# A Mamba layer pair of two batches as one pipeline of eight half-sequence items, in a decoder layer kernel

## The chip, the cores and the metric

One core of one Trainium2 chip runs the whole decoder layer as one program. The metric is the time of one execution on the device in microseconds. The engines are named as the profile names them: PE (TensorE, matrix products and transposes), PEld (its weight loads), DVE (VectorE), ACT (ScalarE), POOL (GpSimd) and SP (SyncE, which only issues transfers here). SBUF is the on-chip memory, PSUM the accumulators of PE (eight banks of 512 float32 per partition).

## What is computed

Four batches of 1024 tokens by 256 features in float32. Each batch goes through two Mamba blocks, a memory attention, a normalisation, a cross-attention over 64 context tokens, another normalisation, and then all batches together through a top-2-of-8 mixture of experts with a last normalisation. What the change touches is the Mamba block and what surrounds it:

```python
def mamba_block(x, in_w, in_b, conv_w, conv_b, xp_w, dt_w, dt_b, A_log, D_ssm, out_w, out_b):
    xz = x @ in_w.T + in_b                      # 256 -> 2 x 512
    xm, res = jnp.split(xz, 2, axis=-1)
    xc = causal depthwise convolution of xm, 4 taps
    xm = silu(xc + conv_b)
    x_dbl = xm @ xp_w.T                         # 512 -> 64 + 16 + 16
    delta = softplus(x_dbl[..., :64] @ dt_w.T + dt_b)
    Bm, Cm = x_dbl[..., 64:80], x_dbl[..., 80:]
    # per token, for 512 channels x 16 states:
    #   h = h * exp(delta * A) + delta * xm * Bm ;  y = sum over states of h * Cm
    y = (y + xm * D_ssm) * silu(res)
    return y @ out_w.T + out_b
out1 = mb(rmsnorm(x, norm1_w));  x1 = x + out1
out2 = mb(rmsnorm(x1, norm2_w)); out2 = memory_attend(out2, ...)
return x1 + out2
```

## The kernel before

Every engine runs its own list of instructions in order, and semaphores tie the lists together; no scheduler reorders anything. The four batches run one after the other. For each, `mamba(b, m)` runs twice (m is the layer), then come the memory attention and the cross-attention, and after the last batch the experts.

A call of `mamba` has three parts. The **preparation** works on all 1024 tokens: the root mean square (L705, L694), scaling (L1308), transposes of the normalised input (L920, drained at L682), the input product (L926), the first convolution tap on ACT (L729) and three on DVE (L1316) out of an SBUF copy `pre`, Silu (L722), the product to rank and B, C (L973), the product to delta (L980), softplus as Abs, Exp, Ln (L745 to L764) with a series for small arguments shared by POOL (L569, L573) and DVE (L1332 to L1351), the product delta times xm (L1327) and its transposes (L998, drained at L799).

The **scan** has 128 chunks: 2 halves of 512 tokens, 16 states, 4 groups of 128 channels. For each state `spread_b` multiplies the transposed delta times xm by B (three of four token tiles on ACT, L779, one on POOL, L582). For each chunk, `fill` transposes 4 tiles into a bank of `psD` (PE, L1012), `decay` computes exp(delta A) into `da_ring` (ACT, L786), DVE scans (L1363) into `h_ring`, POOL multiplies by the broadcast row of C (`weigh_c`, L597), and `add_y` transposes and accumulates in `psA` (PE, L1032). `psD` and `psA` have four banks each, `da_ring` and `h_ring` eight places. `open_y` starts each half's accumulation with 16 products by the diagonal of D_ssm (L1022), after ACT has copied the previous half out (`keep_y`, L792). In the first half POOL also keeps the last state of each chunk (L593).

The **end** transposes y back (L1056), gates it (Silu at L828, product at L1373), and multiplies by out_w (L926, then L1382 or L1385 on DVE).

## Time and profile before

| | us |
|---|---|
| median of 3 runs | 3635.7 (3633.0 to 3639.06) |
| the profiled execution | 3660.78 |
| its span, first to last instruction | 3659.0 |
| busy: PE, DVE, ACT, POOL | 2742.5, 2217.9, 1904.8, 1665.2 |

The span is about 2 us shorter than the profiled execution, which itself is 25 us above the median. Busy time of PE is modelled with overlapping records, so what PE can really issue is read from the distance between starts, not from the mean of one matmul. A line's idle time names whom the engine waited for. The timeline merges equal neighbours; four merged instructions of 0.71 us that span 2.55 us start every 0.61 to 0.64 us.

### The profile page before, as it was taken

The page shows a single profiled execution, that of the slowest core. Times are in us where ns is not written, and L with a number is a line of the kernel's source. Part 1 is how long each engine was busy: PE and PEld are TensorE (multiplying, and loading weights), DVE is VectorE, ACT ScalarE, POOL GpSimd, SP SyncE. Part 2 cuts the span into 40 slices and gives each one's busy share as a digit, 9 for nine tenths or more (in the row PEclk, how much of TensorE's full clock was granted, in tenths as well). Part 3 has the DMA queues.
Part 4 walks back from the last instruction along what each step waited for, and adds up shares of the span by engine and source line. Part 5 has one row for each costly group of instructions (what it writes and reads, how often), then busy time and mean ns, then how long its engine had stood idle before and what let it go on. Part 6 is the DMA issues. An engine that isn't in the chain of part 4 may idle for free.

```text
span 3659.0 us, 44328 instructions
## 1 busy us (share of the span) xinstructions
PE 2742.5 (75%) x15274; PEld 2050.4 (56%) x15275; DVE 2217.9 (61%) x2787; ACT 1904.8 (52%) x3028; POOL 1665.2 (46%) x1723
## 2 busy tenths in 40 slices
PE   5787688877777896687688867777895299999910
PEld 2674576547647754674676547647754166666600
DVE  4894893468668645894893468678643033333347
ACT  5785781378678525785781378678531011111100
POOL 2792791039639602792791039639602501000060
PEclk9898899889989998898899889989996599999955
DMA  5110120001001100110110001001102212111031
GB/s 197 43 51 1 41 64 1 12 18 52 25 18 50 38 1 13 44 50 1 44 61 1 12 18 53 24 18 53 35 1 102 81 62 90 62 63 62 33 93 47
DMA packets 91235, 158.84 MB, mean 43 GB/s; under 512 B 14130, under 2 KB 39986, under 8 KB 91058
## 3 DMA queue, kind: packets, MB, share of 16 engines
q1 hardware_dynamic: 72338, 106.80, 9.4%
q0 software_dynamic: 15392, 47.99, 3.6%
q8 instruction: 104, 1.70, 0.2%
...
q14 instruction: 73, 0.60, 0.1%
...
## 4 chain that ended last, share of the span: by engine, by line
PE 41%; POOL 30%; DVE 11%; issue 8%; ACT 7%; DMA 2%; another core or an unknown queue 1%; DVEq 0%; POOLq 0%; SPq 0%; ACTq 0%
POOL arena L597 25%; PE psD L926 13%; PE psD L1237 7%; PE psA L926 6%; POOL arena L582 4%; PE psD L1114 2%; PE psA L1089 2%; PE psD L1135 2%; DVE arena L1351 2%; PE psA L973 2%; PE psA L1228 1%; DVE arena L1349 1%; PE psA L920 1%; ACT arena L779 1%; DVE arena L1338 1%
## 5 line engine op out<-in xcount | busy, mean ns | idle before, releaser
L597 POOL TENSOR_TENSOR arena<-arena 128x512 f32<-128x512 f32 x1024 | 1091.2, 1092 | 10.7 <-POOL carry L593 0.5
L1012 PE MATMUL psD<-ident,arena 128*128 128x128 f32 x4096 | 651.6, 286 | 274.6 <-ACT arena L779 209.9
L1012 PEld LDWEIGHTS psD<-ident,arena 128*128 128x128 f32 x4096 | 479.1, 146 | 374.0 <-ACT arena L779 273.5
L786 ACT ACTIVATE arena<-arena,negA 128x512 f32<-128x512 f32 x1024 | 662.1, 712 | 12.2 <-DVE arena L1363 11.4
L1363 DVE TENSOR_TENSOR_SCAN arena<-arena,psD 128x512 f32<-128x512 f32 x512 | 581.7, 1200 | 137.8 <-PE psA L1032 81.4
L1032 PE MATMUL psA<-ident,arena 128*128 128x128 f32 x4096 | 617.7, 274 | 19.0 <-POOL arena L597 18.7
L1363 DVE TENSOR_TENSOR_SCAN arena<-arena,carry,psD 128x512 f32<-128x512 f32 x512 | 602.4, 1255 | 37.0 <-PE psA L1032 37.0
L779 ACT ACTIVATE arena<-arena,bc 128x512 f32<-128x512 f32 x768 | 498.0, 712 | 87.4 <-PE psD L1012 86.3
L1032 PEld LDWEIGHTS psA<-ident,arena 128*128 128x128 f32 x4096 | 479.1, 142 | 32.3 <-POOL arena L597 32.3
L926 PE MATMUL psD<-arena 128*128 128x512 f32 (+4 forms) x776 | 336.9, 569 | 43.5 <-POOL strip L545 28.7
L883 ACT ACTIVATE in_w_sb<-in_w_sb 128x512 f32<-128x512 f32 x140 | 88.1, 630 | 457.6 <-DVE in_w_sb L1559 457.6
L926 PE MATMUL psA<-arena,in_w_sb 128*128 128x512 f32 x512 | 251.0, 650 | 84.1 <-ACT bc L769 84.1
L639 POOL DMA_DIRECT2D ys_dram<-arena x70 | 38.0, 543 | 532.8 <-DVE arena L1570 525.1
L682 ACT ACTIVATE arena<-psA 128x512 f32<-128x512 f32 x160 | 90.3, 597 | 319.9 <-PE psA L1089 117.2
L1237 PE MATMUL psD<-arena 128*128 128x256 f32 x1120 | 254.2, 380 | 2.9 <-DVE arena L1565 2.9
L573 POOL TENSOR_TENSOR arena<-arena 128x1024 f32<-128x1024 f32 x32 | 88.2, 2757 | 357.5 <-ACT arena L750 357.5
L1559 DVE TENSOR_TENSOR in_w_sb<-psD,arena 128x512 f32<-128x512 f32 x140 | 96.8, 692 | 244.6 <-PE psD L926 244.6
L582 POOL TENSOR_SCALAR arena<-arena,bc 128x512 f32<-128x512 f32 x256 | 177.0, 692 | 118.1 <-ACT arena L799 118.1
L926 PEld LDWEIGHTS psD<-arena 128*128 128x128 f32 (+1 forms) x776 | 143.1, 194 | 150.8 <-issue 140.7
L926 PEld LDWEIGHTS psA<-arena,in_w_sb 128*128 128x128 f32 x512 | 105.6, 211 | 217.5 <-issue 124.2
L1237 PEld LDWEIGHTS psD<-arena 128*128 128x128 f32 x1120 | 207.3, 190 | 30.1 <-DVE arena L1565 4.8
L555 POOL TENSOR_TENSOR arena<-arena,out_b_sb 128x2048 f32<-128x2048 f32 x4 | 18.0, 4496 | 373.4 <-DMA x_dram<-arena 373.4
...
## 6 DMA issues: line engine op xcount, KB each, us to landing
arena<-c_dram SPq DMA_DIRECT2D x256, 256.0 KB, 3.2
...
arena<-xs_dram SPq DMA_DIRECT2D x71, 128.0 KB
ys_dram<-arena POOLq DMA_DIRECT2D x70, 128.0 KB, 2.0
...
```

The source lines that it names most:

```text
L573: pool.tensor_tensor(series[:, f, :], series[:, f, :], soft_e[:, f, :], ALU.mult)\
L582: pool.tensor_scalar(g[:, v % 2, JS, :], uT[:, t, :], bc[:, t, n:n + 1], 1.0, ALU.mult, ALU.mult).then_inc(b_by_pool, 1)
L597: pool.tensor_tensor(h_ring[:, r % H_SLOTS, :], h_ring[:, r % H_SLOTS, :], c_rows[:, (half * NS + n) % C_SLOTS, :], ALU.mult).then_inc(c_w ...
L682: act.activation(dst, psA[:, bank, 0:width], func, **kw).then_inc(act_drained, 1)
L779: act.activation(g[:, v % 2, j, :], uT[:, t, :], ACT.Copy, scale=bc[:, t, n:n + 1])\
L786: act.activation(da_ring[:, r % DA_SLOTS, :], dt[:, f, half * HALF:(half + 1) * HALF], ACT.Exp, scale=negA[:, f, n:n + 1]).then_inc(da_rea ...
L926: mm = pe.matmul(out_ap, lhs, rhs, start=i == 0, stop=i == len(pairs) - 1)
L1012: mm = pe.transpose(psD[:, r % RING, j * P:(j + 1) * P], g[:, (r // KI) % 2, j, f * P:(f + 1) * P], ident[:, :])
L1032: mm = pe.matmul(psA[:, j, f * P:(f + 1) * P], h_ring[:, r % H_SLOTS, j * P:(j + 1) * P], ident[:, :], is_transpose=True, start=False, sto ...
L1237: mm = pe.matmul(psD[:, 2, 0:D], hidT[:, k, :], w2_sb[:, r, k, :], start=k == 0, stop=k == KH - 1)
L1363: dve.tensor_tensor_scan(h_ring[:, r % H_SLOTS, :], da_ring[:, r % DA_SLOTS, :], psD[:, r % RING, :], 0.0 if half == 0 else carry[:, n, f: ...
L1559: dve.tensor_tensor(hid[:, n * BANK:(n + 1) * BANK], psD[:, n, :], b1_sb[:, r, n * BANK:(n + 1) * BANK], ALU.add).then_inc(hid_ready, 1)
```

## The change

Two batches and their two layers are now one **group** of eight **items** of 512 tokens, in the order batch 0 first half, batch 1 first half, batch 0 second half, batch 1 second half, then the same for the second layer. There are two groups. The scan chunks of all items follow each other without a break: 8 x 64 = 512 chunks per group. On every engine one loop over the chunk number c puts, beside the chunk's own work, pieces of the preparation of the next item (p), of the end of the previous item (k), and of this item's gate product (s), each at fixed positions r = c modulo 64. The loop starts 128 positions early, where only the first item is prepared, and runs 60 positions past the last chunk for the last item's end. The positions, from the tables in the source: bias and normalise on POOL 1; transposes of the input 3, 4; squares of the item after next 4, 5, 8, 9; `keep_y` and `open_y` 6; input products 7, 9, 11, 13, with the convolution's three DVE taps 2, 3 and 4 positions later; all Silus 19; product to rank, B and C 22; B and C transposes 24; delta products 25, 27, 29, 31; y transposes 32, 35, 38, 41 and output products 34, 37, 40, 43; comparison for small arguments 33 to 36; all four logarithms 34; series, replacement, sum and product by xm between 37 and 48 (POOL's share at 35, 36, 42, 43); transposes of delta times xm 43, 44, 50, 51; gate products 46, 48, 52, 54.

The convolution reads the product straight from PSUM, with no `pre` copy; ACT does the last tap with a summed bias, and a halo of 3 columns from the earlier half is added by small DVE instructions. Chunks now have two banks of `psD`; the other two serve everything that is not scan. `da_ring` has six places. The root of the mean square is exp(-0.5 ln), and normalising is POOL's. Layer 2's output goes to DRAM tile by tile and comes back for the memory attention, as x does for the sum. The attention parts keep their instructions and now run twice in a row, one batch after the other. In the experts' entry, both loads of the stored x2 rows now wait for the last normalisation; one used to be issued earlier.

```diff
         CHUNKS = NS * KI
-        RUN = 2 * CHUNKS
-        DA_SLOTS = H_SLOTS = 8
-        C_SLOTS = 4
+        ITEMS = 8
+        GROUPS = B // 2
+        RUN = ITEMS * CHUNKS
+        TAIL = 60
+        DA_SLOTS, H_SLOTS, C_SLOTS = 6, 8, 4
+        FILL_BANKS = 2
...
+        SQUARE = [4, 5, 8, 9]
...
+        STAGES = (("mo", MO, -1, "dve", 1), ("xnT", XNT, 1, "act", 1), ("in", IN, 1, "dve", 4),
+                  ("xd", XD, 1, "act", 1), ("bcT", BCT, 1, "act", 1), ("z", Z, 1, "dve", 2), ("turn", TURN, -1, "dve", 1),
+                  ("uT", UT, 1, "act", 1), ("gate", GATE, 0, "act", 1))
...
+            def keep_o2(i, j):
+                u, q, m, h = item_at(i % ITEMS)
+                sp.wait_ge(bg_by_dve, taken("mo", i, j))
+                sp.dma_start(o2_dram[u, h * JT + j], o2_tile[:, j % 2, :]).then_inc(o2_stored[j % 2], 16)
...
+                def soften(i, f):
+                    n = i * KI + f
+                    pool.wait_ge(soft_exp, n + 1)
+                    pool.wait_ge(slope_ready, n + 1)
+                    pool.tensor_tensor(series[:, f % 2, :], series[:, f % 2, :], soft_e[:, f, :], ALU.mult)\
+                        .then_inc(cubic_step, 1)
...
+                def keep_y(i):
+                    act.wait_ge(summed, (i + 1) * CHUNKS)
+                    if i == 0:
+                        act.wait_ge(xs_zeroed, ZEROED)
+                    for j in range(JT):
+                        act.activation(yT[:, j, :], psA[:, j, :], ACT.Copy).then_inc(y_kept, 1)
...
+                def decline(i, f):
+                    n = i * KI + f
+                    act.wait_ge(bg_full, filled("z", i, f))
+                    act.activation(soft_e[:, f, :], psD[:, bg_bank("z", i, f), :], ACT.Abs, bias=dt_b_sb[:, f:f + 1])\
+                       .then_inc(soft_abs, 1)
+                    act.wait_ge(soft_abs, n + 1)
+                    act.activation(soft_e[:, f, :], soft_e[:, f, :], ACT.Exp, scale=-1.0).then_inc(soft_exp, 1)
...
+                def logarithms(i):
+                    for f in range(KI):
+                        act.wait_ge(soft_exp, i * KI + f + 1)
+                        if f == 0:
+                            act.wait_ge(dt_ready, KI * i)
+                        act.activation(soft_ln[:, f, :], soft_e[:, f, :], ACT.Ln, bias=1.0).then_inc(soft_log, 1)
...
+                def claim_bg(name, i, j):
+                    q = bg_at[name, i, j][0]
+                    if q >= 2:
+                        by, count, time = bg_jobs[q - 2]
+                        pe.wait_ge(bg_by_act if by == "act" else bg_by_dve, count)
...
+                def project_in(name, i, f, column):
+                    pe.wait_ge(bg_by_act, taken("xnT", i, KD - 1))
+                    claim_bg(name, i, f)
+                    product(psD[:, bg_bank(name, i, f), :],
+                            [(in_w_sb[:, k, column * P:(column + 1) * P], xnT[:, i % 2, k, :]) for k in range(KD)])\
+                        .then_inc(bg_full, 1)
...
-                    if r >= RING:
-                        pe.wait_ge(scanned, blk * RUN + r - RING + 1)
...
+                    if c >= FILL_BANKS:
+                        pe.wait_ge(scanned, g0 * RUN + c - FILL_BANKS + 1)
...
+                def open_y(i):
 
                     for j in range(JT):
-                        if half == 1:
-                            pe.wait_ge(y_kept, blk * TT + j + 1)
+                        if i > i0:
...
-                for r in range(FILL_AHEAD):
-                    fill(r)
-                for r in range(RUN + SUM_AFTER):
-                    if r + FILL_AHEAD < RUN:
-                        fill(r + FILL_AHEAD)
...
+                for c in range(-2 * CHUNKS, RUN + TAIL):
+                    r, k, s, p, p2 = when(c)
+                    if 0 <= c + FILL_AHEAD < RUN:
+                        fill(c + FILL_AHEAD)
+                    if 0 <= c - SUM_AFTER < RUN:
+                        add_y(c - SUM_AFTER)
+                    if k is not None and r in MO:
+                        leave(i0 + k, MO.index(r))
+                    if p is not None and r in XNT:
+                        turn_xn(i0 + p, XNT.index(r))
+                    if p is not None and r in IN:
...
-                for f in range(KI):
-                    dve.wait_ge(tap0_ready, blk * KI + f + 1)
-                    for tap in range(1, TAPS):
-                        if tap > 1:
-                            dve.wait_ge(conv_step, blk * ((TAPS - 1) * KI) + ((TAPS - 1) * f + tap - 1))
-                        dve.scalar_tensor_tensor(xm[:, f, :], pre[:, f, tap:tap + T], conv_w_sb[:, f, tap:tap + 1],
-                                                 xm[:, f, :], op0=ALU.mult, op1=ALU.add).then_inc(conv_step, 1)
...
+                def convolve(i, f, tap):
+                    n = (i * KI + f) * TAPS
+                    u, q, m, h = item_at(i - i0)
+                    cols = TAPS - 1 - tap
+                    bank = psD[:, bg_bank("in", i, f), :]
+                    if cols == 1:
+                        dve.wait_ge(bg_full, filled("in", i, f))
+                        dve.wait_ge(tap0_ready, i * KI + f + 1)
+                    else:
+                        dve.wait_ge(conv_step, n + cols - 1)
+                    last = dve.scalar_tensor_tensor(xm[:, f, cols:], bank[:, 0:HALF - cols], conv_w_sb[:, f, tap:tap + 1],
+                                                    xm[:, f, cols:], op0=ALU.mult, op1=ALU.add)
+                    last.then_inc(conv_step, 1)
+                    if cols == TAPS - 1:
+                        dve.wait_ge(conv_step, n + cols)
+                        if h == 0:
+                            dve.wait_ge(halo_ready, 5)
+                        else:
+                            dve.wait_ge(halo_ready, 5 * (g0 * 4 + m * 2 + u + 2))
+                        which = 0 if h == 0 else 1 + u
+                        dve.tensor_tensor(xm[:, f, 0:cols], xm[:, f, 0:cols], halo_sum[:, which, f, :], ALU.add).then_inc(conv_step, 1)
+                        dve.tensor_copy(halo[:, 1 + u, f, :], bank[:, HALF - cols:HALF]).then_inc(bg_by_dve, 1)
+                def add_dt_b(i, f):
+                    bank = bg_wait("z", i, f)
+                    dve.wait_ge(soft_abs, i * KI + f + 1)
+                    dve.tensor_scalar(dt[:, i % 2, f, :], bank, dt_b_sb[:, f:f + 1], 0.0, ALU.add, ALU.max).then_inc(bg_by_dve, 1)
...
+                def scan(c):
+                    q, n, f = chunk(c)
+                    u, layer_half, m, h = item_at(q)
+                    if f == 0 and h == 1:
+                        dve.wait_ge(carried, (g0 * 4 + m * 2 + u) * NS + n + 1)
+                    if c >= H_SLOTS:
+                        dve.wait_ge(summed, g0 * RUN + c - H_SLOTS + 1)
+                    dve.wait_ge(da_ready, g0 * RUN + c + 1)
+                    dve.wait_ge(dbu_full, g0 * RUN + c + 1)
+                    dve.tensor_tensor_scan(h_ring[:, c % H_SLOTS, :], da_ring[:, c % DA_SLOTS, :], psD[:, c % FILL_BANKS, :],
+                                           0.0 if h == 0 else carry[:, u, n, f:f + 1], ALU.mult, ALU.add)\
+                       .then_inc(scanned, 1)
+                for c in range(-2 * CHUNKS, RUN + TAIL):
+                    r, k, s, p, p2 = when(c)
+                    if 0 <= c < RUN:
...
+                        sum_halo(halo[:, 1 + u, :, :], halo_sum[:, 1 + u, :, :], 5 * (g0 * 4 + m * 2 + u + 1) + 4)
+                    if k is not None and r - 1 in MO:
+                        leave(i0 + k, MO.index(r - 1))
+                    if p is not None:
+                        for f in range(KI):
+                            for tap in range(TAPS - 1):
+                                if r == IN[f] + 4 - tap:
+                                    convolve(i0 + p, f, tap)
...
+                    if p is not None:
+                        for f in range(KI):
+                            if r == SMALL[f]:
+                                find_small(i0 + p, f)
+                            if r == SERIES[f]:
+                                expand(i0 + p, f)
+                            if r == REPLACE[f]:
+                                replace(i0 + p, f)
+                            if r == FINISH[f]:
+                                finish_dt(i0 + p, f)
+                            if r == TIMES[f]:
```

PE, where an item's accumulation is opened. Before, in the middle of a block (L1012 fills a chunk's bank, L1032 adds a chunk to y, L1022 is `open_y`):

```order
L1032 MATMUL psA<-ident,arena 128x128 x4
L1012 MATMUL psD<-ident,arena 128x128 x4
L1022 MATMUL psA<-diag_d,arena 128x128 x16
L1032 MATMUL psA<-ident,arena 128x128 x4
L1012 MATMUL psD<-ident,arena 128x128 x4
```

The same place now, positions 4 to 9 of an item (L1152 fills, L1172 adds, L1162 is `open_y`, L1107 transposes the next item's input, L1056 is its input product):

```order
L1107 MATMUL psD<-ident,arena 128x128 x4
L1152 MATMUL psD<-ident,arena 128x128 x4
L1172 MATMUL psA<-ident,arena 128x128 x4
L1152 MATMUL psD<-ident,arena 128x128 x4
L1162 MATMUL psA<-diag_d,arena 128x128 x16
L1172 MATMUL psA<-ident,arena 128x128 x4
L1152 MATMUL psD<-ident,arena 128x128 x4
L1172 MATMUL psA<-ident,arena 128x128 x4
L1056 MATMUL psD<-arena,in_w_sb 128x512 x2
L1152 MATMUL psD<-ident,arena 128x128 x4
L1172 MATMUL psA<-ident,arena 128x128 x4
```

The input product, which stood in the preparation, now stands one position behind `open_y` between two fills.

DVE, where softplus is finished. Before, in the preparation, with 64 and 64 scans behind it (L1338 series, L1327 product by xm, L1349 replacement, L1351 sum, L1363 scan):

```order
L1338 SCALAR_TENSOR_TENSOR arena<-arena 128x1024
L1327 TENSOR_TENSOR arena<-arena 128x1024
L1349 COPY_PREDICATED arena<-arena 128x1024
L1351 SCALAR_TENSOR_TENSOR arena<-arena 128x1024
L1327 TENSOR_TENSOR arena<-arena 128x1024
L1363 SCALAR_TENSOR_TENSOR arena<-arena,psD 128x512 x64
L1363 SCALAR_TENSOR_TENSOR arena<-arena,carry,psD 128x512 x64
```

Now, positions 37 to 40 (L1580 scan, L1553 series, L1511 output of the previous item, L1561 replacement, L1501 gating of the previous item, L1565 sum, L1569 product by xm):

```order
L1553 SCALAR_TENSOR_TENSOR arena<-arena 128x512
L1580 SCALAR_TENSOR_TENSOR arena<-arena,carry,psD 128x512
L1511 TENSOR_TENSOR arena<-psD,arena 128x256
L1561 COPY_PREDICATED arena<-arena 128x512
L1553 SCALAR_TENSOR_TENSOR arena<-arena 128x512
L1580 SCALAR_TENSOR_TENSOR arena<-arena,carry,psD 128x512
L1501 TENSOR_TENSOR arena<-psD,arena 128x512
L1565 TENSOR_TENSOR arena<-arena 128x512
L1561 COPY_PREDICATED arena<-arena 128x512
L1580 SCALAR_TENSOR_TENSOR arena<-arena,carry,psD 128x512
L1569 TENSOR_TENSOR arena<-arena 128x512
```

Two or three pieces of half the width now stand between one scan and the next.

## Rows read from the trace of the kernel before

**Rows 1.** Windows: stretch, busy us (count) of PE, PEld, DVE, ACT, POOL; PE clock, DMA.

```profile
38.20:116.90 78.70, 55.62 (x162) 27.73 (x163) 49.80 (x50) 50.81 (x65) 18.81 (x8) 0.83 0.24 84
116.90:282.00 165.10, 133.15 (x1072) 119.82 (x1070) 148.11 (x128) 140.17 (x224) 156.54 (x173) 0.97 0.15 46
282.00:311.00 29.00, 21.80 (x104) 18.41 (x104) 7.92 (x12) 12.25 (x27) 3.40 (x3) 0.88 0.00 1
585.00:713.00 128.00, 112.90 (x496) 73.75 (x496) 53.56 (x127) 39.77 (x81) 6.42 (x2) 0.95 0.00 1
2765.00:3659.00 894.00, 601.29 (x2578) 423.01 (x2578) 330.85 (x762) 126.91 (x242) 186.91 (x231) 0.83 0.20 71
```

**Rows 2.** Timeline (start, us, engine, line, operation [idle before]) of a first half's scan.

```profile
195.24 4.55 DVE L1363 TENSOR_TENSOR_SCAN arena<-arena,psD 128x512 f32<-128x512 f32 x4 [0.58 <-PE psA L1032]
...
196.34 0.60 PE L1032 MATMUL psA<-ident,arena 128*128 128x128 f32 x4
196.35 2.14 POOL L597 TENSOR_TENSOR arena<-arena 128x512 f32<-128x512 f32 x2
196.78 0.60 PE L1012 MATMUL psD<-ident,arena 128*128 128x128 f32 x4
...
199.27 2.55 ACT L786 ACTIVATE arena<-arena,negA 128x512 f32<-128x512 f32 x4
...
201.48 2.14 POOL L597 TENSOR_TENSOR arena<-arena 128x512 f32<-128x512 f32 x2
```

**Rows 3.** Timeline of a second half, around `open_y`, and later.

```profile
209.72 3.74 PE L1022 MATMUL psA<-diag_d,arena 128*128 128x128 f32 x32
...
213.34 0.70 POOL L582 TENSOR_SCALAR arena<-arena,bc 128x512 f32<-128x512 f32 x1
...
213.99 5.96 DVE L1363 TENSOR_TENSOR_SCAN arena<-arena,carry,psD 128x512 f32<-128x512 f32 x5 [3.66 <-PE psA L1032]
...
218.23 0.70 POOL L582 TENSOR_SCALAR arena<-arena,bc 128x512 f32<-128x512 f32 x1
```

**Rows 4.** Groups by line: operation, count, busy us, mean ns, idle.

```profile
L1439 DVE SCALAR_TENSOR_TENSOR arena<-psD,arena 128x512 f32<-128x512 f32 x16 | 11.1, 691 | 74.4 <-PE psD L926 74.4
L1570 DVE TENSOR_TENSOR arena<-psD,arena 128x256 f32 x70 | 29.7, 425 | 217.7 <-PE psD L1237 217.7
```

**Rows 5.** Timeline of ACT at the end of the block's scan.

```profile
283.89 2.07 ACT L792 ACTIVATE arena<-psA 128x512 f32<-128x512 f32 x4 [12.79 <-PE psA L1032]
285.97 1.28 ACT L828 ACT_TABLE_LOAD   x1
287.26 2.95 ACT L828 ACTIVATE arena<-arena 128x1024 f32<-128x1024 f32 x3
```

**Rows 6.** Timeline of PE: products of preparation and end (two records per product).

```profile
59.77 2.74 PE L926 MATMUL psA<-arena,in_w_sb 128*128 128x512 f32 x6
62.34 7.03 PE L973 MATMUL psA<-arena,xp_w_sb 128*96 128x512 f32 x16
69.30 7.13 PE L980 MATMUL psD<-arena,dt_w_sb 64*128 64x512 f32 x16
292.85 15.08 PE L926 MATMUL psD<-out_w_sb,arena 128*128 128x256 f32 x64
```

**Rows 7.** Timeline: POOL and DVE in the preparation's softplus.

```profile
88.83 2.92 POOL L573 TENSOR_TENSOR arena<-arena 128x1024 f32<-128x1024 f32 x1
...
89.45 3.38 DVE L1338 SCALAR_TENSOR_TENSOR arena<-arena 128x1024 f32<-128x1024 f32 x1
...
99.20 1.21 DVE L1338 SCALAR_TENSOR_TENSOR arena<-arena 128x1024 f32<-128x1024 f32 x1
```

**Rows 8.** The chain that ended last: start, us, what; at batch change and experts' entry.

```profile
712.72 4.26 DMA x_dram<-arena
717.24 5.25 DVE arena L1308 x4
...
2765.25 16.75 DMA arena<-x_dram
```

1300 lines of the change are left out of this document (688 added, 612 removed).

## The prediction, made before the changed kernel was run

> **What bounds the kernel now.** I read the windows first, to see which stretches there are. Batch 0 begins at 38.2 us; its first block is a preparation of 78.7, a scan of 165.1 and an end of 29.0 us, 272.8 together, and the attentions take 128.0 [rows 1]. The next batch starts scaling at 717.24, after a store of 4.26 us that it waits for [rows 8]. The four batches fill 38.2 to 2765, 2726.8 us, and the experts 894 [rows 1]. In the scan every engine is busy for most of the time (POOL 156.5 of 165.1, DVE 148.1, ACT 140.2), in the preparation none is for more than 56 of 78.7, and in the end only PE is [rows 1]. So the change has two stretches in which each engine waits for the others, and wants to lay them beside the scan. What that is worth depends on how much room the scan leaves, so I read the timeline next for the distance between starts.
>
> Per chunk the scan costs: POOL, from 196.35 to 201.48, 5.13 us for four chunks in a first half, and from 213.34 to 218.23, 4.89 in a second [rows 2, 3], so 1.25 on average. DVE, four scans in 4.55 where one lasts about 1.2, is a start every 1.12, and 1.18 in second halves (five in 5.96), so 1.15 [rows 2, 3]. ACT starts every 0.64 (four in 2.55) and has seven operations for four chunks (four decays, three of spread_b), 1.12 [rows 2]. PE starts the next four transposes 0.44 later (196.34, 196.78), 0.87 a chunk, though its busy column looks full [rows 2]. POOL is the bound, and DVE's 0.58 before the scan is POOL seen through `add_y` [rows 2]. A pure scan item of 64 chunks takes 80 us (POOL); half a block now takes 136.4. The room is at most 56 us an item, if the side work fits.
>
> **The change, part by part.** First the side work of one item, by engine.
>
> DVE: 12 convolution taps and 4 delta drains and 4 gatings from PSUM at 0.64 (0.69 less the overlap of neighbours) [rows 4], 12.8; 4 outputs at 0.4, half-width, 1.6; 16 operations from SBUF (series, replacement, sum, product by xm) at 0.6, half of 1.21 [rows 7], 9.8; 4 comparisons at 0.4, 1.6; 12 to 17 tiny halo operations, which no row shows, between 0 and 0.6 each, as they may queue behind a POOL instruction: I take 2.5. Sum 28.3, and with the scans 73.4 it is 102.
> ACT: keep_y 2.1, 8 Silus 4.2 [rows 5]; 31 more full-width operations (2 input transposes, 4 taps, 4 gates, 8 Abs and Exp, 4 slopes, 4 logarithms, the rank drain, 4 drains of transposes) at 0.52 to 0.64, 17.7; squares, roots and the small drain 2.5; four table loads at 1.28 [rows 5], 5.1. Sum 32, with 72 for the chunks 104.
> PE: 8 products from the input at two of 0.86 (0.43 a record, two records each), 13.8; rank 3.5, delta 3.6, output 7.5 (16, 16 and 64 records for two items) [rows 6]; 10 groups of transposes at 0.44; `open_y` 3.7 [rows 3]. Sum 36.5, with 56 for the chunks 92.
> POOL: series 4.3, normalising 1.6, bias 1.1 on average; sum 7, with 80 for the chunks 87.
>
> So no engine's sum is under 102, and the four sums can't all be hidden behind each other, for the rings let an engine be ahead by a few chunks only: ACT by four to six (`da_ring`), POOL behind by six, PE ahead of DVE by two banks. The side work is bunched, with DVE's and ACT's bunches at different positions. I therefore add the item up in stretches, each at its fullest engine, and give back what a ring can carry over.
> - Positions 0 to 8: PE opens y at 6 and has the first input product at 7. Before, DVE waited 3.66 for `open_y` with four banks [rows 3]; it is the same wait now, and the input product of 1.73 right behind it adds under 1. DVE 10.4 and 4.4 of waiting, 15. ACT's 15.7 here is carried partly by its ring.
> - 9 to 17: DVE, 9 scans 10.3, taps 7.7, halo 2, and drains, 21. ACT has 12.4, PE 13.
> - 18 to 36: ACT, 19 chunks 21.4, Silus with two loads 6.8, Abs and Exp 4.6, slopes, logarithms with two loads 5.9, small ones 1.1, 39.8; it enters with its ring full, about 5 us, so 34 to 35. DVE has 29, and PE's rank product (3.5 in one position) and delta products stop it for 3 more, which hides under ACT.
> - 37 to 48: DVE, 12 scans 13.8, 16 SBUF operations 9.8, gatings and outputs 2.5, 26; with 4 to 5 for POOL in its way (below), 31. PE has 19.
> - 49 to 63: DVE 17.3; two gate products of 1.73 each stop it for about 1.2, 20. POOL's 18.8 is just under.
>
> That makes 121 us an item, against 136.4. The bounds are 102 (DVE's sum alone) and 134 (each stretch at its fullest with ACT's 5 and another 8 not given back). I stay nearer the middle, since `open_y`, a bunch of 3.7, was hardly hidden by buffers in the row of before, and there are some ten such bunches now.
>
> Per group: the lead, the first item's preparation with nothing beside it, between 39 (half of 78.7) and 79; 48, since its chain of dependent steps does not halve. Seven items at 121, less 7 for the first, which has no predecessor to finish, 840. The last, with no preparation beside it: 80, less a little for a second half, plus `open_y` 3.7 and gating, 87. The tail: POOL finishes its six chunks 6, keep_y and Silus 6, four times transposes, gating, product, output one behind the other 13.5, against 29.0 for twice the tokens [rows 1]; then the store and load of layer 2's output, nearest row 4.26 for 1 MB [rows 8], 6; 32. Group: 1007.
>
> The rest: attentions 4 x 128 [rows 1], as before; that the second batch's may begin under the first one's normalisation, I count at nothing. The sum of x, x1 and the output on POOL is about 11 us and is needed some 40 us later by the read product, so the returning transfers are hidden behind the memory products; if they weren't, 4 x 4.3. One wait of 4.3 for a store remains of three. A second 1 MB at the start, 3. At the experts' entry the chain had 16.75 for 2 MB [rows 8]; now the first 1 MB is read only there, 8 more. SP issues the same number of C rows; the stores of output tiles stand 4 rows apart behind steps that are done by then, nothing. The smaller number of zero-filling transfers is hidden as before.
>
> Sum: 38.2 + 3 + 2 x 1007 + 4 x 128 + 4.3 + 894 + 8 = 3473.5 of span, 185 less than 3659.0. The profiled execution was 25 above the median; I take the 185 off the median and get 3450.
>
> Where POOL gets in the way: in the preparation DVE's L1338 took 3.38 when POOL's L573 had begun 0.6 before it, and 1.21 with POOL still [rows 7]; 89.45 plus 3.38 less 1.21 is 91.62, when POOL's instruction was just about over. An instruction with two SBUF inputs waits for POOL's to end. POOL is busy nearly always now. But each multiply by C starts when a scan ends, and DVE's own next instruction is already in line then; mostly POOL will wait, and it has the room. So 4 to 5 us an item for DVE, of up to 25.
> The Trainium skill, "GPSIMD Engine Reference", section 1, "Specifications", says that GpSimd's SBUF interfaces are shared with VectorE where that has two SBUF inputs or runs in a two-port mode. By that rule the scan and the taps from PSUM are free of it, and this trace agrees: POOL keeps its 1.07 beside scans.
>
> **Rivals.**
> 1. The rings carry nearly everything and an item costs little over the fullest engine's sum, 110. For it: side work is a quarter to a third of each engine, and spread. Against: the 3.66. It gives 14 x 11 less, 3296.
> 2. Slower, by the shared way into SBUF. DVE's 20 SBUF operations at 33 to 48, and the halo's 4, each find a multiply by C of 1.05 just begun and wait for all of it: 25 us an item instead of 5. Item 141, time 3450 + 14 x 20 = 3730. It decides from 13 us more an item (185 / 14), or, with the 4 to 5 already counted, 0.75 of waiting on each of the 24. For it: the 3.38 [rows 7], and POOL at 95% of the scan [rows 1]. Against: the order in which the two are released.
> 3. ACT's four changes of table an item cost more than the load, and ACT sets the pace from 18 to 36. If each costs twice the row's 1.28, it is 5.5 us an item, 3450 + 77 = 3527. Against: keep_y ends at 285.96, the load runs from 285.97, and the Silu starts at 287.26, 1.29 later [rows 5].
> The Trainium skill, "ScalarE: Activation LUTs", section "What ACT_TABLE_LOAD costs", has 1283 ns for the load and about 1380 more for a drain; by it this rival would be right, but the trace shows only the first part.
> 4. The pipeline does not run as one, and each item waits at its border for its predecessor's steps: 56 us of room not used, about 3640. Against: layer 2's first item needs the item four before it.
>
> **Numbers.** Forecast 60%, rival 1 17%, rival 3 10%, rival 2 10%, rival 4 3%. The forecast's own range is 3380 to 3520 (item 116 to 126). The range 3310 to 3610 leaves out rival 2, the lower half of rival 1 and some of rival 4. A difference of 0.2% is about what a measurement of this kernel tells from none. Faster: the forecast, rivals 1 and 3 and little else, 86%; the same 2%; slower, rival 2 and part of rival 4, 12%.
>
> **What would show it.** In the new profile the scans of a group are one unbroken row: 64 starts take 116 to 126 us in the middle items and 85 to 90 in the last. DVE has its longest waits at position 8 or 9, behind PE's `open_y` (3 to 4 us), and spans for L1553, L1565 and L1569 near 0.6 with a few above 1. ACT is without idle time between Silu and logarithms. Busy times: DVE near 2250, POOL near 1700, PE's and ACT's about as before. I would be wrong if the middle items take under 112 or over 130, if L1553's mean is over 1.2 us (rival 2), or if the gap behind a table load exceeds 0.3 us (rival 3).

## The result, and the profile after

The changed kernel takes 3805.65 us (median of four runs, 3798.4 to 3838.24) against 3636.36, a ratio of 1.048 with a 95% interval of 1.042 to 1.054. It is slower by 169 us where 185 less were forecast, and outside the range of 3310 to 3610. The profiled execution has a span of 3804.0.

The windows of the kernel after answer to [rows 1]. Columns: stretch and its length, busy us (count) of PE, PEld, DVE, ACT, POOL, then PE's clock, DMA share, GB/s. The rows are the lead from 38.2 to the first scan, item 0, item 3, item 7 (the last of the group), from there to the second group's first scan, and the experts:

```profile
38.20:90.10 51.90, 24.16 (x70) 10.96 (x69) 28.93 (x45) 29.79 (x51) 9.75 (x8) 0.75 0.34 134
90.10:216.20 126.10, 101.39 (x593) 76.98 (x591) 106.13 (x109) 99.36 (x165) 99.09 (x97) 0.87 0.11 30
507.30:651.10 143.80, 111.33 (x669) 85.61 (x670) 111.75 (x117) 102.71 (x171) 102.63 (x90) 0.92 0.10 30
1079.70:1182.70 103.00, 87.21 (x612) 71.05 (x612) 82.28 (x72) 74.50 (x118) 90.28 (x80) 0.98 0.13 42
1182.70:1539.70 357.00, 278.02 (x1126) 176.53 (x1127) 139.95 (x305) 112.60 (x203) 37.51 (x23) 0.86 0.09 29
2910.00:3804.00 894.00, 602.92 (x2602) 423.95 (x2601) 339.57 (x790) 127.08 (x243) 192.20 (x231) 0.84 0.21 72
```

Read the lengths first. Everything that is not an item came as forecast: the lead is 51.9 (48 + 3), the stretch between the groups 357 where tail, two attentions, a store and a lead make 340, and from the last scan (2630.1) to the end 1174 where 1190 were counted. The first scans of group 0's items start at 90.1, 216.2, 363.2, 507.3, 651.1, 791.3, 933.9 and 1079.7: item 0 takes 126, the six middle ones 140 to 147, the last 103. Eight items are 1092.6 in the first group and 1090.4 in the second, where the sum had 927 each: 329 too long, and the rest is right to 1.5 us in total (3473.5 + 329 + 1.5 = 3804.0). The whole miss is in the items. In item 3 no engine is busy for more than 112 of 143.8: they wait for each other. (In the medians the miss is 25 us larger, 3805.65 against 3450: the profile before lay 25 above its median, which I took off, and the profile after lies at its median.)

By my five stretches, the mean of the twelve middle items (worked out from the starts of the scans and DVE's instructions between them; the busy column counts the short overlap of neighbours twice):

```
positions   forecast   measured   DVE busy   DVE idle, and what ended most of it
0 to 8       15         20.1       13.3       7.0   PE's sum (L1172) 6.9
9 to 17      21         21.9       22.6       1.1   ACT's tap (L850) 1.1
18 to 36     34 to 35   42.8       31.5      12.7   L1172 7.7, output product (L1056) 2.4, Abs (L866) 1.9
37 to 48     31         36.5       33.3       5.6   output product (L1056) 5.6
49 to 63     20         22.4       18.6       3.9   L1172 3.9
```

The groups by line of the kernel after (line, engine, operation, shapes, count; busy us, mean ns of one; idle before it):

```profile
L703 POOL TENSOR_TENSOR arena<-arena 128x512 f32<-128x512 f32 x1024 | 1319.2, 1314 | 10.5 <-POOL carry L699 0.2
L1561 DVE COPY_PREDICATED arena<-arena 128x512 f32<-128x512 uint8 x64 | 76.8, 1199 | 0.1
L1565 DVE TENSOR_TENSOR arena<-arena 128x512 f32<-128x512 f32 x64 | 70.8, 1106 | 0.0
L1553 DVE SCALAR_TENSOR_TENSOR arena<-arena 128x512 f32<-128x512 f32 x64 | 59.7, 933 | 0.0
L1548 DVE TENSOR_SCALAR arena<-arena 128x512 uint8<-128x512 f32 x64 | 48.1, 759 | 0.0
L1569 DVE TENSOR_TENSOR arena<-arena 128x512 f32<-128x512 f32 x64 | 46.8, 731 | 0.1
L1538 DVE TENSOR_TENSOR arena<-arena,halo_sum 128x3 f32<-128x3 f32 x64 | 32.3, 505 | 2.2
```

Two things stand here that [rows 2, 7] did not lead me to. The multiply by C has the form that it had before and takes 1314 ns; the same row of the kernel before says 1092. And an addition of three columns takes 505. DVE's five kinds of operations from SBUF, 16 x 20 of them, are busy for 302.2 us. One instruction and its shortest, median and longest time, from the views of the single lines:

```profile
L703 POOL TENSOR_TENSOR arena<-arena x1024: 1252/1276/1824, 95.4 to 2634.2; 128x512 f32<-128x512 f32 x171
L1561 DVE COPY_PREDICATED arena<-arena x64: 702/1313/1807, 72.9 to 2496.7; 128x512 f32<-128x512 uint8 x64
L1538 DVE TENSOR_TENSOR arena<-arena,halo_sum x64: 161/164/1206, 47.3 to 2423.0; 128x3 f32<-128x3 f32 x64
```

With each of the five at its shortest (702, 654, 657, 394, 656) they would take 196.0, and the halo's sums 10.3 instead of 32.3: 128 us of waiting, 8.0 an item. The timeline of item 3 shows such a wait (DVE's three columns stand from 544.22 until POOL's multiply, begun at 544.13, is over), and later an output:

```profile
544.13 1.28 POOL L703 TENSOR_TENSOR arena<-arena 128x512 f32<-128x512 f32 x1
544.22 1.20 DVE L1538 TENSOR_TENSOR arena<-arena,halo_sum 128x3 f32<-128x3 f32 x1
545.34 0.15 DVE L1539 COPY halo<-psD 128x3 f32<-128x3 f32 x1
...
594.44 1.89 PE L1056 MATMUL psD<-out_w_sb,arena 128*128 128x256 f32 x8
596.37 0.42 DVE L1511 TENSOR_TENSOR arena<-psD,arena 128x256 f32<-128x256 f32 x1 [1.14 <-PE psD L1056]
596.71 1.32 DVE L1561 COPY_PREDICATED arena<-arena 128x512 f32<-128x512 uint8 x1
597.93 1.74 DVE L1553 SCALAR_TENSOR_TENSOR arena<-arena 128x512 f32<-128x512 f32 x1
```

The output's own 0.42 I had in the sum. That DVE stands 1.14 before it, since in DVE's order it comes one position behind the product and nothing else may pass, I had at nothing.

### The profile page after: what moved, and what is told of

The parts are those of the page before. It is cut to its first block, busy times and chain, and to the rows that moved or that the text cites. A ratio compares the mean times of both kernels' runs of the same rounds, so it can differ in the third digit from the quotient of the medians.

```text
span 3804.0 us, 45601 instructions
## 1 busy us (share of the span) xinstructions
PE 2862.1 (75%) x15274; PEld 2092.5 (55%) x15275; DVE 2344.1 (62%) x3190; ACT 1933.3 (51%) x3239; POOL 1890.0 (50%) x1807
## 4 chain that ended last, share of the span: by engine, by line
PE 49%; DVE 21%; issue 12%; ACT 8%; POOL 8%; DMA 2%; SPq 0%; another core or an unknown queue 0%; DVEq 0%; POOLq 0%; ACTq 0%
PE psD L1056 16%; PE psD L1378 6%; PE psD L1152 6%; DVE arena L1580 6%; POOL arena L703 6%; PE psA L1172 4%; DVE arena L1528 3%; DVE arena L1561 2%; PE psD L1121 2%; PE psD L1255 2%; PE psA L1056 2%; PE psA L1230 2%; DVE arena L1565 2%; ACT arena L894 2%; ACT arena L904 1%
## 5 line engine op out<-in xcount | busy, mean ns | idle before, releaser
L703 POOL TENSOR_TENSOR arena<-arena 128x512 f32<-128x512 f32 x1024 | 1319.2, 1314 | 10.5 <-POOL carry L699 0.2
L1152 PE MATMUL psD<-ident,arena 128*128 128x128 f32 x4096 | 702.8, 298 | 450.2 <-DVE arena L1580 372.5
L1152 PEld LDWEIGHTS psD<-ident,arena 128*128 128x128 f32 x4096 | 493.4, 150 | 713.6 <-DVE arena L1580 425.4
L904 ACT ACTIVATE arena<-arena,negA 128x512 f32<-128x512 f32 x1024 | 717.0, 711 | 54.2 <-DVE arena L1580 53.8
L1580 DVE TENSOR_TENSOR_SCAN arena<-arena,carry,psD 128x512 f32<-128x512 f32 x512 | 637.5, 1269 | 150.1 <-PE psA L1172 136.4
L1580 DVE TENSOR_TENSOR_SCAN arena<-arena,psD 128x512 f32<-128x512 f32 x512 | 609.9, 1210 | 160.7 <-PE psA L1172 141.6
L1172 PE MATMUL psA<-ident,arena 128*128 128x128 f32 x4096 | 661.2, 287 | 9.5 <-POOL arena L703 9.5
L894 ACT ACTIVATE arena<-arena,bc 128x512 f32<-128x512 f32 x768 | 546.2, 712 | 174.9 <-PE psD L1152 174.6
L1172 PEld LDWEIGHTS psA<-ident,arena 128*128 128x128 f32 x4096 | 520.9, 150 | 13.1 <-POOL arena L703 13.1
L1056 PE MATMUL psD<-arena 128*128 128x512 f32 (+4 forms) x776 | 335.7, 568 | 45.4 <-POOL strip L647 30.5
L1056 PE MATMUL psD<-arena,in_w_sb 128*128 128x512 f32 x512 | 258.1, 629 | 14.6 <-DVE halo L1539 12.4
L1056 PEld LDWEIGHTS psD<-arena 128*128 128x128 f32 (+1 forms) x776 | 142.6, 194 | 152.1 <-issue 142.2
L1770 DVE TENSOR_TENSOR arena<-psD,arena 128x256 f32 x70 | 29.7, 425 | 218.0 <-PE psD L1378 218.0
L1528 DVE SCALAR_TENSOR_TENSOR arena<-psD,conv_w_sb,arena 128x511 f32<-128x511 f32 (+2 forms) x192 | 139.9, 729 | 36.1 <-ACT arena L850 35.6
```

What stands on the lines that cost most here:

```text
L703: pool.tensor_tensor(h_ring[:, c % H_SLOTS, :], h_ring[:, c % H_SLOTS, :], c_rows[:, v % C_SLOTS, :], ALU.mult).then_inc(c_weighed, 1)
L894: act.activation(g[:, v % 2, j, :], uT[:, i % 2, j, :], ACT.Copy, scale=bc[:, i % 2, j, n:n + 1])\
L904: act.activation(da_ring[:, c % DA_SLOTS, :], dt[:, i % 2, f, :], ACT.Exp, scale=negA[:, f, n:n + 1]).then_inc(da_ready, 1)
L1056: mm = pe.matmul(out_ap, lhs, rhs, start=i == 0, stop=i == len(pairs) - 1)
L1152: mm = pe.transpose(psD[:, c % FILL_BANKS, j * P:(j + 1) * P], g[:, (c // KI) % 2, j, c % KI * P:(c % KI + 1) * P], ident[:, :])
L1172: mm = pe.matmul(psA[:, j, f * P:(f + 1) * P], h_ring[:, c % H_SLOTS, j * P:(j + 1) * P], ident[:, :], is_transpose=True, start=False, sto ...
```

## The experiments

Ratios are to the kernel before, timed beside each run on the same chip, each with its 95% interval; differences of ratios are turned into us with 3636. Their own intervals are 8 to 9 us either way, 14 to 16 for the differences of e5 to e8 against e3, and 23 for e1 against the changed kernel. Where it matters I give beside them what the two traces have for the 16 items. Three theories stood at the start. D: the slower multiply comes from where its operands lie. In the changed kernel the ring of states begins 5120 words behind the rows of C, a multiple of 512; before it was 22542, 14 more than one. (A place of either ring is 512 words, so each pair of operands lies at this distance give or take a multiple of 512.) L: DVE waits for POOL at the way into SBUF. O: order and bunches, that is, PE or ACT does more in one position than one scan covers, and DVE stands.

**Operand distance.** e1 on the changed kernel:

```diff
         da_ring = by_ring(carve(6 * HALF))
+        carve(14)
         h_ring = by_ring(carve(8 * HALF))
```


> The changed kernel with 14 unused words between the ring of decays and the ring of states, so that a state and its row of C no longer lie a multiple of 512 words apart (5120 becomes 5134; before it was 22542). Theory 1, operand distance: the multiply by C (L703) goes from a mean of 1314 ns and a minimum of 1252 back to about 1080 to 1110, POOL's busy time falls by about 200 us, the stretch of positions 49 to 63 of a middle item goes from 22.4 to about 20, 37 to 48 from 36.5 to about 35, and the time falls by 50 to 110, to 3695 to 3755. Theory 2, the multiply is slower because DVE, ACT or DMAs are busier beside it: it stays at 1250 or more and the time is the changed kernel's, 3800. In neither does the whole difference to my forecast go away.

1.0343 (1.0326 to 1.0361), 51 us less than the changed kernel. The gain lies elsewhere than expected: the positions 49 to 63 went from 22.4 to 22.0 only, the positions 0 to 8 from 20.1 to 18.5. e2 on the kernel before:

```diff
+        h_flat = carve(2 * KI * HALF)
+        da_flat = carve(2 * KI * HALF)
         xnT_flat = carve(KD * (T + 1))
...
-        h_flat = carve(2 * KI * HALF)
...
-        da_flat = carve(2 * KI * HALF)
```


> The kernel before with its two rings carved ahead of the normalised input, so that a state and its row of C lie a multiple of 512 words apart (8192 instead of 22542); nothing else. Theory 1, operand distance: its multiply by C (L597) goes from 1092 to about 1260 ns, the chunk's 1.25 us to 1.43, and with POOL the bound of 1024 chunks the time goes from 3636 to 3790 to 3825. Theory 2, busier neighbours: nothing changes, 3630 to 3645.

1.0502 (1.0484 to 1.0519), 183 us slower with not one instruction changed. The multiply's line in the kernel before, in e2 and in e1:

```profile
L597 POOL TENSOR_TENSOR arena<-arena x1024: 1078/1092/1122, 121.9 to 2613.4; 128x512 f32<-128x512 f32 x171
```
```profile
L597 POOL TENSOR_TENSOR arena<-arena x1024: 1255/1279/1366, 121.3 to 2781.9; 128x512 f32<-128x512 f32 x171
```
```profile
L704 POOL TENSOR_TENSOR arena<-arena x1024: 1081/1095/1562, 98.1 to 2586.4; 128x512 f32<-128x512 f32 x171
```

D is shown from both sides. The multiplies took 189 us more in e2, and the time followed by 183, since POOL bounds that kernel; in the pipeline they took 194 less in e1 and gave 51 (42 in the items of the two traces), because the item is held by other things.

These two runs leave open whether the distance decides or the place of one operand. Rows of the traces settle it. The changed kernel adds to one tile (`base`, from word 4096) first `xin`, which begins 4096 or 2048 words away, and then `o2`, 33042 away, which is 2 more than a multiple of 16:

```profile
L725 POOL TENSOR_TENSOR arena<-arena x4: 4516/4518/4522, 1220.3 to 2801.7; 128x2048 f32<-128x2048 f32 x4
L728 POOL TENSOR_TENSOR arena<-arena x4: 3807/3810/3811, 1224.9 to 2806.3; 128x2048 f32<-128x2048 f32 x4
```

The output is the same tile both times, so its place is not the cause. And L573 in the kernel before has both its tiles 14 words behind a multiple of 512, but 4096 apart: it takes 2347 ns at the shortest, and 2347 in e2, where both lie on a multiple. From the shortest times of the multiplies at 512 and the sums at 2048 columns I estimate 2343 for a slow product of 1024 and 1988 for a quick one, so it is slow in both. The distance decides.

**Sums earlier.** e3 on e1; e3 is the base of e5 to e9:

```diff
-        FILL_AHEAD, SUM_AFTER, DECAY_AHEAD, WEIGH_AFTER = 2, 6, 4, 4
+        FILL_AHEAD, SUM_AFTER, DECAY_AHEAD, WEIGH_AFTER = 2, 5, 4, 4
...
-        XB, NORM, KEEP_Y = 1, 1, 6
+        XB, NORM, KEEP_Y = 1, 1, 5
```


> The padded kernel with PE's sums one position earlier (5 instead of 6 behind the scan, and the copy of y with it). Theory A, cover: a scan waits for the sum of eight chunks before, which stands behind PE's fill and its background product, so that DVE has one scan of cover, 1.27 us, for everything that PE does in a position; with one position more it has two. Then DVE's idle time in front of scans (6.9, 7.7 and 3.9 us of an item in the positions from 0, 18 and 49 on) falls to about half, an item by 5 to 9 us and the time by 60 to 110 against the padded kernel. Theory B, PE now waits for POOL's multiply instead: the time stays within 15 us of the padded kernel's or rises, and PE has idle time behind POOL.

1.0310 (1.0291 to 1.0329): 12 us, with intervals that touch. Theory A is wrong, and both signs of theory B came: under 15 us, and PE's wait for POOL's multiply, 2.1 us in a group of e1, is 15.8 in e3. But the larger part is in neither: the waits did not halve, they changed their name. DVE's idle time in the positions 0 to 8, 6.3 behind PE's sums, is now 6.6 behind PE's fills. PE itself is late, whatever it is asked for first.

**The products that open y**, left out on e1:

> The padded kernel without the products that open y with D times u (64 of 128x128 for a block; this part of the result is left out), but with the wait for the copy of y. It prices that bunch. If the 20.1 us of the positions 0 to 8 are the 3.7 of these products standing behind the copies of y, the stretch falls to 15 to 16.5, an item by about 4 and the time by about 55 to 65 against the padded kernel. If the wait for the copy of y by itself is what costs, the stretch stays above 18.

1.0258 (1.0241 to 1.0275), 31 us against e1, half of what I expected. The first stretch went from 18.5 to 16.5: 2 of the 3.7 us were on the path.

**Outputs later.** e5 on e3:

```diff
-        STAGES = (("mo", MO, -1, "dve", 1), ...
+        STAGES = (("mo", MO, -1, "dve", 2), ...
...
-                    if k is not None and r - 1 in MO:
-                        leave(i0 + k, MO.index(r - 1))
+                    if k is not None and r - 2 in MO:
+                        leave(i0 + k, MO.index(r - 2))
```


> The kernel of the run before (padded, sums one position earlier; 3734 us) with one thing moved: DVE takes an output (L1512, L1517) two positions behind PE's product instead of one. Theory O: DVE stands in its order in front of a product that PE only starts after the scan before it, and waits for nearly all of its 1.89 us, 1.45 on average, four times an item (5.8 us in the positions 37 to 48, 0.9 in 18 to 36), which my sum had at nothing. Then DVE's wait for the product falls from 6.7 to under 2 us an item, the stretch 37 to 48 from 35.9 to about 31 to 32, and the time by 50 to 85. Rival: the wait only moves, as PE is late for its fills anyway: DVE then waits at the next scan for PE's transposes instead and the time falls by under 20.

1.0212 (1.0179 to 1.0246), 36 us against e3 (28 in the items of the traces). DVE's waits of one group's scans, e3 first, then e5 (waiting line, what it waited for: us, times, longest):

```profile
DVE arena L1517 <- PE psD L1057: 29.9, 16, 3.9
DVE arena L1512 <- PE psD L1057: 26.6, 16, 3.1
```
```profile
DVE arena L1517 <- PE psD L1057: 15.2, 10, 3.7
DVE arena L1512 <- PE psD L1057: 4.9, 5, 1.4
```

36 us less waiting here in one group, but only 18 came out. In the positions 37 to 48 DVE idled 1.9 instead of 5.8, and its SBUF operations there grew from 15.2 to 17.3: while it had stood for PE, POOL's multiplies had gone by. Theory and rival each hold by about half.

**Without the multiplies.** e6 on e3; the factor C is left out:

```diff
-                    pool.tensor_tensor(h_ring[:, c % H_SLOTS, :], h_ring[:, c % H_SLOTS, :],
-                                       c_rows[:, v % C_SLOTS, :], ALU.mult).then_inc(c_weighed, 1)
+                    pool.sem_inc(c_weighed, 1)
```


> The padded kernel with the earlier sums, without POOL's 1024 multiplies by C (this factor is left out of the result; the semaphore is raised when the scan is done). It prices POOL as a neighbour and as a bound. Theory L, the shared way: DVE's operations from SBUF fall to their shortest (L1562 from 1114 to about 700 ns, L1554 from 917 to 660, L1566 and L1570 from 886 and 866 to 660, the comparison from 985 to 400, halo sums from 474 to 160), 7 to 8 us an item, and the time falls by 80 to 120. Theory P, POOL's multiply also stops PE's sums: then the positions 49 to 63 fall from 20.9 to 19 too, and the time by over 130. If neither holds, it falls by under 40.

0.9828 (0.9794 to 0.9862), 175 us against e3. In the traces the 16 items fell by 146 and a middle item from 140.3 to 129.4. Not all of the 175 is the pipeline's: with other values the experts had 69 tiles instead of 70. Three of the groups:

```profile
L1561 DVE COPY_PREDICATED arena<-arena 128x512 f32<-128x512 uint8 x64 | 47.1, 735 | 0.1
L1565 DVE TENSOR_TENSOR arena<-arena 128x512 f32<-128x512 f32 x64 | 45.6, 712 | 0.0
L1580 DVE TENSOR_TENSOR_SCAN arena<-arena,carry,psD 128x512 f32<-128x512 f32 x512 | 625.4, 1263 | 115.7 <-PE psD L1152 86.2 <-ACT arena L904 24.4 <-PE psA L1172 4.8
```

L is shown: the five kinds of SBUF operations fell from 299.4 us (e3) to 216.8, the halo's sums to 161 in the median and 165 at most, the positions 37 to 48 from 35.9 to 30.7 us. The scan kept its 1263 (1263 in e3), so it had not waited for POOL. Of theory P the total came (over 130), not the place: the positions 49 to 63 went from 20.9 to 20.6 only, and 3.1 of the 11 us an item in the positions 0 to 8.

**One table.** e7 on e3, Silu and the logarithms replaced by copies:

> The padded kernel with the earlier sums, where Silu and both logarithms are replaced by copies of the same shape, so that ACT changes its table no more (these functions are left out of the result). It prices four loads of 1.28 us an item with what stands behind them. Theory T: ACT carries the positions 18 to 36, and DVE's idle time there (12.0 us) is its bunch: the stretch falls from 42.4 by 4 to 6, the time by 55 to 85. Rival: ACT has slack there behind its ring and the time falls by under 20.

1.0179 (1.0144 to 1.0215), 48 us against e3. This hides a part: with other values the tokens are spread otherwise over the experts, which had 73 tiles instead of 70 (L1760, two for a tile, has 146 instructions and not 140), and took 24 us longer than in e5 and e8 on the same chip. In the traces the 16 items fell by 68, 4.3 each for four loads of 1.28, and the positions 18 to 36 went from 42.4 to 38.9. Theory T holds, with about 70 us (48 and 24).

**Silus one position later.** e8 on e3:

```diff
-        SILU = 19
+        SILU = 20
```


> The padded kernel with the earlier sums, with ACT's block of eight Silus (7 us with its two loads) at position 20 instead of 19, which puts the third spread by B of the next row ahead of it. Theory G: PE waits 2.7 to 4 us for that spread in the middle of its fills, as ACT is ahead by only one row of g; then PE's wait for ACT (4.2 us an item) goes below 2, the stretch 18 to 36 falls by 2 to 3 us and the time by 25 to 45. Rival: the decays behind the block become the late ones instead (their ring has six), and nothing changes within 10 us.

1.0152 (1.0113 to 1.0191), 57 us against e3 for one number, by ratios whose interval goes from 42 to 73; in the traces the items fell by 41, and the positions 18 to 36 from 42.4 to 40.0. Theory G holds. PE's waits for ACT's spread by B, over one group, e3 and then e8:

```profile
PE psD L1153 <- ACT arena L895: 32.2, 9, 4.9
```
```profile
PE psD L1153 <- ACT arena L895: 7.9, 4, 3.3
```

ACT's block of Silus had stood between two of the three spreads of one row of g. PE needed the third, was late, and DVE with it. One position gives more than half of what leaving out all table loads gives (41 against 68 in the items): a good part of the block's price is what it stands in front of.

**All three moves of order.** e9: the last two, and four opening products in each of the first four positions instead of 16 in one.

```diff
-                    if c % CHUNKS == 0:
-                        open_y(i0 + q)
+                    if n == 0:
+                        open_y(i0 + q, f)
```


> Three small moves of order together on the padded kernel with the earlier sums: the Silus at position 20, DVE's outputs two positions behind their product, and the 16 products that open y laid over the first four chunks of an item (four in each position) instead of all 16 ahead of the first. The first two gave 58 and 36 us when each stood alone, against 1.031 of the kernel before. Theory: bunches on PE and ACT longer than one scan are what stops DVE, so the third gives 1.5 to 2.5 us an item more in the positions 0 to 8 (DVE's idle time there 6.2 to about 4), and the three add up to 90 to 130: 1.000 to 1.010 of the kernel before. Rival: waits hand over to each other, as with the outputs alone, where DVE's wait fell by 4.8 us and the item by 2.5: together they give under 70, and it stays above 1.015.

1.0097 (1.0080 to 1.0114), 77 us against e3, between theory and rival. A new wait came: ACT's tap, which overwrites the convolved input, now waits for the last opening product, and DVE for the tap, 27.9 us in a group where e5 had 10.1.

**Pairs, and one halo sum.** e10 on e9: the five kinds of SBUF operations on two channel blocks at once. e11 on e10: one sum of 4 x 3 columns instead of four.

```diff
-                    dve.copy_predicated(soft_ln[:, f, :], is_small[:, f, :], series[:, f % 2, :]).then_inc(replaced, 1)
+                    dve.copy_predicated(soft_ln[:, f - 1:f + 1, :], is_small[:, f - 1:f + 1, :], series[:, 0:2, :]).then_inc(replaced, 2)
...
-                        dve.tensor_tensor(xm[:, f, 0:cols], xm[:, f, 0:cols], halo_sum[:, which, f, :], ALU.add).then_inc(conv_step, 1)
+                            dve.tensor_tensor(xm[:, :, 0:cols], xm[:, :, 0:cols], halo_sum[:, which, :, :], ALU.add)\
+                               .then_inc(conv_step, KI)
```


> The kernel of the run before with DVE's five kinds of operations from SBUF (comparison, series, replacement, sum, product by xm) done for two channel blocks at a time, 10 of 128x1024 an item instead of 20 of 128x512. Theory L, each such operation waits for one multiply of POOL's that has just begun, whatever its own size: half the waits go, 3 us of the 6 that were found when the multiplies were left out, so an item falls by 2.5 to 4 and the time by 35 to 60. Rival: the way is shared in proportion to the elements, or POOL's instructions slip in more often beside the longer ones: the time stays within 15 us.

> The kernel of the run before with the four additions of three columns each at a convolution's edge (L1538, 505 ns on average where the shortest is 161) made one of 4 x 3 columns at the end. Theory L: three of four waits for POOL go, about 1.0 us an item and 0.5 for the three instructions, in the positions 9 to 17, where DVE is the bound: 1 to 1.5 us an item, 14 to 21 in all. Rival: ACT or PE take over as the bound there and it gives under 7.

e10 0.9928 (0.9911 to 0.9944), 61 us; e11 0.9840 (0.9824 to 0.9856), 32 more. The five kinds' busy time fell from 324.1 (e9) to 238.2 in e10; ten fewer starts an item explain 1.2 of the 5.4 us an item (1294 for a pair at its shortest against twice 702), fewer waits the other 4.2. Half the instructions over the same elements waited 3.8 us an item instead of 8.0, so each instruction pays the wait, and not each element. e11 gave more than its instructions' time (25.1 us of halo sums became 2.8), which I can't place.

**Distances again, and the input products.** e12 is e11 without the 14 words, e13 with 64 instead; e14 and e15 are e11 with `IN = [8, 10, 12, 14]` and `[9, 11, 13, 15]`; e16 is e15 with 16 words, e17 e15 with a second `carve(14)` ahead of `series`.

> The kernel of the run before (all moves; 0.984 of the kernel before) without its 14 unused words: state and row of C are 5120 words apart again. Theory: the multiply goes from 1.11 to about 1.30 us. If POOL's slack still hides most of it, as in the changed kernel (58 us there), the time rises by 40 to 70; if POOL is nearer the bound now (128.5 us an item against 140), by 80 to 130. Rival: nothing, because a multiply that blocks DVE's wide operations longer is hidden by the fewer of them: under 20.

> The same kernel with 64 unused words instead of 14, a distance of 5184 words, which is a multiple of 64 and not of 512. If the slow distance is any multiple of 64 words, the multiply takes 1.26 us or more and the time is that of the run without padding. If only multiples of a larger power of two are slow, it takes 1.08 to 1.11 and the time is within 8 us of the kernel with 14 words. I hold both for equally likely.

> The kernel with 14 words and all moves, with the four input products one position later (8, 10, 12, 14 instead of 7, 9, 11, 13). ACT's tap may only start when the last product that opens y has read the convolved input, and since these lie in four positions it waits 2.8 us an item for it, and DVE 4.0 for the tap. Theory: the wait falls by the one position, 1.2 us or more an item, the time by 15 to 30. Rival: the wait moves to the Silus at position 20, and nothing changes within 8 us.

> The same with the input products two positions later (9, 11, 13, 15). Theory: DVE's wait for the first tap falls from 4.0 to under 1.5 us an item and the time by 25 to 45 against the kernel with the products at 7. Rival: the convolution now ends at position 19, so that the Silus at 20 and the rank product at 22 are late, ACT's bunch moves into the positions 22 and on, and the time is that of the one-position move or worse.

> The fastest kernel so far (0.9794 of the kernel before, input products at 9, 11, 13, 15) with 16 unused words instead of 14, a distance of 5136 words, a multiple of 16 and not of 64. If any multiple of 16 is slow, the multiply's median goes from 1.093 to about 1.275 us and the time rises by 30 to 45; if it has to be a multiple of 32 or 64, it stays at 1.09 and the time within 8 us. Since 64 was slow I give the first 6 in 10.

> The fastest kernel so far with 14 more unused words ahead of the two tiles of the series, so that POOL's product of a series and its exponential (L676, 64 of 128x512, 4096 words apart) is off a multiple of 64 words as well. Theory, operand distance: its shortest time goes from 1.25 to 1.08 us, 64 x 0.17 is 11 us of POOL's time, mostly hidden, and the time falls by 0 to 12. Rival: the product keeps 1.25, and the distance matters only where the output lies on an input's place in some other way.

```
run   distance   multiply, shortest/median/longest   ratio (95%)
e12   5120       1251/1274/2365                      0.9940 (0.9923 to 0.9957)
e13   5184       1252/1275/2368                      0.9928 (0.9911 to 0.9944)
e11   5134       1081/1093/2169                      0.9840 (0.9824 to 0.9856)
e14   5134       1079/1092/2189                      0.9798 (0.9781 to 0.9814)
e15   5134       1078/1092/2153                      0.9794 (0.9777 to 0.9810)
e16   5136       1254/1276/2378                      0.9876 (0.9859 to 0.9892)
e17   5134       1083/1094/2172                      0.9778 (0.9761 to 0.9794)
```

A multiple of 64 words is as slow as one of 512, and so is 5136, a multiple of 16 only. POOL's other product, in e15 and in e17, where its operands went from 4096 to 4110 words apart:

```profile
L676 POOL TENSOR_TENSOR arena<-arena x64: 1260/1282/2247, 72.7 to 2257.4; 128x512 f32<-128x512 f32 x64
```
```profile
L677 POOL TENSOR_TENSOR arena<-arena x64: 1084/1094/2071, 73.3 to 2250.7; 128x512 f32<-128x512 f32 x64
```

The distance costs 36 us in the quick version (e12 against e11), 32 in e13 and 30 in e16, just under the 40 to 70 and far from the 80 to 130 for POOL nearer the bound. Against the changed kernel's 51, with 23 either way, no difference can be told. e14 gave 15; e15 gave no more than e14, so its rival holds. e17's 6 us against e15 lie within the intervals; its product was quicker as expected. It is the fastest, 2.2% under the kernel before, with the idea of the change whole in it; its middle items take 122 to 130, 126.2 on average.

## Why the prediction was wrong

**Bounds of the kernel before, the room of 56 us, lead, tail, experts:** right, within 17 us in each place. POOL as the bound of the scan was shown by e2, where 189 us on POOL gave 183.

**The step that failed** is the adding up in stretches: "I therefore add the item up in stretches, each at its fullest engine, and give back what a ring can carry over", 121 us, with 134 as the upper bound. The middle items took 143.6, over that bound. Of the waits between engines the sum held only 4.4 for `open_y`, 4 to 5 for POOL and 1.2 for the gate products. It had at nothing those for the output product, for ACT's spread and for PE's fills and sums that come late, and DVE stood idle for 30 us of an item. DVE's and ACT's sums were near: 102 against 112 with waits for POOL inside, and 104 against 103; PE's 92 against 111 by the busy column; POOL's 87 against 103, of which the operand distance is 12 (64 x 0.19). Item 0, which has no predecessor to gate and put out, and was counted with 114, took 15.0, 21.9, 34.4, 31.8 and 23.0, close to the five of the forecast, which were meant with a predecessor. What makes a middle item longer is the predecessor's side work and its place in the order:
- The outputs were four times 0.4. DVE also stood 2.0 before each, 8.0 an item (2.4 and 5.6 in the table above). e5 gave back 2.3 of it; the rest came out as other waits.
- The positions 18 to 36 were to be ACT's with its ring full on entry, 34 to 35; they took 42.8. ACT's Silus stood in front of a spread that PE needed (e8, 3.6 an item by the ratio, 2.6 by the traces). The 5 us that I gave back for ACT's ring are not there, for 42.8 is more than the 39.8 without them. The reason that I see is argued and not shown: the decays are four ahead, but g is only two rows deep.
- Positions 0 to 8, 15 forecast: DVE idles 7.0, not 4.4, as the copy of y, the opening and the input product follow each other. e4 prices the opening at 2.

A rival that no run separates is PE's clock. The granted clock was 0.97 in the scan before [rows 1], and is 0.92 in item 3. Worked out from the trace's clock records, a middle item has 24.5 us at the lower of the two levels (1.2 GHz), where PE's transposes start every 213 ns and not every 109, and DVE stands behind PE for 34% of that time against 16% of the rest. In item 3 the clock fell at 517.7, 548.5, 586.0 and 599.7, and PE had been busy for 6.1, 6.1, 6.7 and 6.5 of the 10 us before, against 77% in the whole item. So the lower clock may be the result of the waits as much as their cause; in e11, with fewer waits, 12.2 us are left of the 24.5. The costs of the transposes and of `open_y` in my sum came from the scan before, nearly all of it at the higher level.

**POOL in the way:** "mostly POOL will wait", 4 to 5 an item. It was 8.0, and POOL's multiplies cost 10.9 us of a middle item in all by e6. The rule was read rightly from [rows 7], the frequency wrongly: DVE's SBUF operations come in a row, and behind each a waiting multiply begins. POOL's multiply is the longer for it too, 1477 on average in the positions 37 to 48.

**The price of the multiply by C:** "this trace agrees: POOL keeps its 1.07 beside scans". It does beside scans; but the price belongs to a place in memory, and the change moved it. 0.19 x 1024, of which 51 us were on the path (e1). The carving of the arena stood in the kernel after, and I didn't read it for this.

**Rivals.** Rival 2 named the end, 3730 and slower, and an item of 141; that is partly luck. Its mechanism is shown by e6 and e10, but at 0.33 us for each of the 24 operations (128 us / 384), not 1.05, under the 0.75 from which it would have decided alone, and its sign, a mean of L1553 over 1.2 us, did not come (0.93). It took D and O beside it. Rival 3 (whose 5.5 us an item should have been 5.1, four times 1.28) is refuted by e7 (4.3 an item for all four loads, where it had 10) and by ACT's timeline in item 3, which has no gap on either side of a load:

```profile
587.65 0.28 ACT L829 ACTIVATE inv_rms<-mean_sq,eps_sb 128x4 f32<-128x4 f32 x1
587.95 1.28 ACT L904 ACT_TABLE_LOAD   x1
589.24 0.72 ACT L904 ACTIVATE arena<-arena,negA 128x512 f32<-128x512 f32 x1
```

Rival 1 is refuted by the middle items. Of rival 4 nothing is seen: each stretch of a middle item, not its border, holds part of the loss.

These shares don't add up to 22 us an item, because the waits stand in for each other, as e5 and e9 show. About 5 us an item over the forecast's 121 remain in e17. DVE still idles 93.0 us in a group behind PE's fills there, and no run took that apart.
